# Convolution pieces one slot earlier in an eight-block kernel of convolution and gated network

## The reference

```python
y = irfft(rfft(u, n) * rfft(K, n), n)[..., :L] + u * D
y = y * (arange(L) < length)
q = lambda v: clip(v, -448, 448).astype(float8_e4m3fn).astype(float32)   # all input scales are 1
h = silu(q(y) @ gate_w.T * gate_scale) * (q(y) @ up_w.T * up_scale)      # 512 -> 1376
out = x + q(h) @ down_w.T * down_scale                                   # 1376 -> 512
```

## Time and profile before

| | us |
|---|---|
| median of 3 runs | 326.05 |
| the profiled execution | 326.16 |
| its span | 324.4 |
| TensorE (PE) busy | 310.2 (96%) |
| VectorE (DVE) busy | 303.4 (94%) |
| ScalarE (ACT) busy | 206.3 (64%) |

### The profile page before, as it was taken

The page is one execution under the profiler, slowest core; times in us unless marked ns, Lnnn a source line. Parts: engine busy times, 40 slices in busy tenths (PEclk is TensorE's granted clock), DMA queues, the critical chain, the costliest instruction groups (busy, mean ns, idle before and its releaser), DMA issues.

```text
span 324.4 us, 4763 instructions
## 1 busy us (share of the span) xinstructions
PE 310.2 (96%) x1567; PEld 162.7 (50%) x1593; DVE 303.4 (94%) x464; ACT 206.3 (64%) x318; POOL 12.5 (4%) x20
## 2 busy tenths in 40 slices
PE   1999899999999999999999999999999999989996
PEld 1557554545455554555455544555455454534444
DVE  6989999999999999999998999989998999989784
ACT  4839788278755777476844868366863959364540
POOL 2031000000001000010001000010001000010010
PEclk9999999999999999999999999999999999999999
DMA  5779999400001690077302780067401650051028
GB/s 203 169 179 226 259 277 379 174 1 0 2 0 17 131 359 15 1 129 266 122 0 26 154 337 1 0 116 249 154 0 16 132 242 1 0 100 31 0 34 226
DMA packets 14014, 38.38 MB, mean 118 GB/s; under 512 B 1470, under 2 KB 6558, under 8 KB 11052
## 3 DMA queue, kind: packets, MB, share of 16 engines
q1 hardware_dynamic: 8412, 26.58, 23.1%
q0 software_dynamic: 5584, 11.57, 20.5%
HBM read 33.90 MB, written 15.81 MB: 153 GB/s over the span
## 4 chain that ended last, share of the span: by engine, by line
PE 75%; DVE 16%; issue 4%; ACT 3%; DMA 2%; DVEq 0%; ACTq 0%; SPq 0%
PE gate_ps L535 19%; PE up_ps L535 18%; PE down_ps L491 17%; PE y_ps L477 16%; DVE hv L834 3%; DVE yq L818 3%; DVE yt L807 2%; DVE hq L851 2%; DVE ht L842 2%; PE y_ps L576 1%; DVE ym L799 1%; PE down_ps L576 1%; DMA toep<-kpad_scratch 1%; PE gate_ps L456 1%; PE y_ps L459 1%
## 5 line engine op out<-in xcount | busy, mean ns | idle before, releaser
L392 ACT ACTIVATE sil<-gate_ps,fac 128x512 f32<-128x512 f32 (+1 forms) x88 | 59.7, 680 | 67.8 <-PE gate_ps L535 66.8
L535 PE MATMUL gate_ps<-yq,wg 128*128 128x512 bf16 (+3 forms) x365 | 88.1, 362 | 2.7 <-DVE hv L834 2.4
L535 PE MATMUL up_ps<-yq,wu 128*128 128x512 bf16 (+3 forms) x367 | 88.4, 363 | 0.3
L477 PE MATMUL y_ps<-xt,toep 128*128 128x512 f32 (+3 forms) x256 | 80.4, 434 | 0.5 <-DMA toep<-kpad_scratch 0.5
L491 PE MATMUL down_ps<-wd,hq 128*128 128x512 bf16 (+1 forms) x295 | 76.8, 379 | 0.8
L834 DVE SCALAR_TENSOR_TENSOR hv<-up_ps,fac,sil 128x512 f32<-128x512 f32 (+1 forms) x88 | 65.6, 745 | 8.2 <-ACT sil L392 6.6
L375 ACT ACTIVATE hc<-hv 128x1024 f32<-128x1024 f32 (+1 forms) x48 | 47.1, 980 | 20.9 <-DVE hq L851 19.8
L477 PEld LDWEIGHTS y_ps<-xt,toep 128*128 128x128 f32 x256 | 47.2, 190 | 21.4 <-issue 2.9
L535 PEld LDWEIGHTS gate_ps<-yq,wg 128*128 128x128 bf16 x372 | 35.6, 100 | 43.7 <-ACT sil L392 4.0
L842 DVE SCALAR_TENSOR_TENSOR ht<-hc,hv 128x1024 f32<-128x1024 f32 (+1 forms) x48 | 54.2, 1129 | 1.9 <-ACT hc L375 1.8
L535 PEld LDWEIGHTS up_ps<-yq,wu 128*128 128x128 bf16 x372 | 36.3, 100 | 38.3
(11 more groups left out here) (149 smaller groups left out, 113.0 us busy)
## 6 DMA issues: line engine op xcount, KB each, us to landing
xt<-in_xT SPq DMA_DIRECT2D x8, 1024.0 KB, 7.6
out<-in_x SPq DMA_DIRECT2D x7, 1024.0 KB, 5.7
out<-res POOLq DMA_DIRECT2D x7, 1024.0 KB, 7.8
toep<-kpad_scratch SPq DMA_DIRECT2D x6, 1024.0 KB, 9.8
toep<-kpad_scratch SPq DMA_DIRECT2D x8, 256.0 KB, 4.3
wd<-in_down POOLq DMA_DIRECT2D x1, 1280.0 KB, 21.6
xt<-in_x SPq DMA_DIRECT2D x1, 1024.0 KB, 7.2
out<-xt SPq DMA_DIRECT2D x3, 256.0 KB, 3.1
```

What stands on the lines that cost most here:

```text
L392: nc.scalar.activation(sil[b][0:w, :], gate_ps[b][0:w, :], ACT.Silu, scale=fac[0:w, S_GATE:S_GATE + 1]).then_inc(silu_done, 1)
L477: last = nc.tensor.matmul(y_ps[h % 2][:, d * P:L], toep[par][:, h, d * P:(d + 1) * P], xt[par][:, h, 0:L - d * P], start=(d == 0), stop=(d ...
L535: mm = nc.tensor.matmul(ps[b][0:w, cols], wt[:, k, c * P:c * P + w], yq[par][:, version, k, cols], start=(k == 0), stop=(k == LB - 1))
```

## The change

It moves instructions and alters none:

- `CONV_PLAN`: all pieces of the convolution stand one slot earlier. A block's convolution begins in slot 6 and ends in slot 4; the last piece of channel 1 falls into slot 10, the first of channel 2 into slot 0.
- For block 1 the first piece of channel 2 stands in the start-up, ahead of the last channel's matmuls.
- VectorE: the mask of the first channel two blocks ahead goes from slot 10 to slot 9; the sum of y's last channel from slot 8 to slot 9, behind the tenth product.
- ScalarE: the two copies of K's last group stand before the fourth channel's work of block 0 and not behind it.
- SyncE: the copy of block 0's x is issued behind the loads of block 3.

```diff
--- before.py
+++ after.py
@@ -254,8 +254,8 @@
             load_x_t(2, 0)
             sp.wait_ge(k_stored[2], 16)
             load_toep(2, 0)
+            next_conv(3, 1)
             copy_x(0, 0)
-            next_conv(3, 1)
             copy_x(1, 1)
             with sp.Fori(0, (NBLK - 4) // 2) as j:
                 for par in range(2):
@@ -406,12 +406,13 @@
 
             act.wait_ge(scales_ready, 1)
             for h in range(HB):
+                if h == HB - 1:
+                    copy_k(2)
                 if h:
                     scale_y(0, h)
                 else:
                     act.wait_ge(ym_done, 1)
                 magnitude_y(0, h)
-            copy_k(2)
             scale_y(1, 0)
             magnitude_y(1, 0)
             slots(0, 0, None, True, 2)
@@ -508,7 +509,7 @@
             def beside(g, par, half, c, down, ahead):
 
                 for step, h, distances in CONV_PLAN.get(c, ()):
-                    if step <= ahead and (down or (step, h) != (1, 1)):
+                    if step <= ahead and (down or c):
                         conv(g + step, (par + step) % 2, half + (1 if step == 2 else par), h, distances)
                 if down:
                     down_part(g - 1, 1 - par, c)
@@ -549,6 +550,7 @@
             by_channel(1)
             conv(1, 1, 0, 1, [0, 1, 3, 2])
             by_channel(2)
+            conv(1, 1, 0, 2, [0])
             by_channel(3)
             pe.wait_ge(middle_in, 32)
             slots(0, 0, 0, False, 2)
@@ -910,9 +912,9 @@
                         clip_y(g + 1, 1 - par, ROUND_PLAN[c])
                     if c == 9 and c in plan:
                         rounded(PAIRS * g + plan[c], g, par, plan[c])
+                    if ahead == 2 and c == 9:
+                        mask_y(g + 2, 0)
                     if c == CH - 1:
-                        if ahead == 2:
-                            mask_y(g + 2, 0)
                         if PAIRS - 3 not in plan.values():
                             clip(PAIRS * g + PAIRS - 4, par, PAIRS - 4)
                         rounded_sum(m - 1, PAIRS - 2)
@@ -969,15 +971,14 @@
 
 
 CONV_PLAN = {
-    7: [(2, 0, [0])], 8: [(2, 0, [1, 3])], 9: [(2, 0, [2]), (2, 1, [0])], 10: [(2, 1, [1, 3])],
-    0: [(1, 1, [2])], 1: [(1, 2, [0])], 2: [(1, 2, [1, 3])], 3: [(1, 2, [2]), (1, 3, [0])],
-    4: [(1, 3, [1, 3])], 5: [(1, 3, [2])],
+    6: [(2, 0, [0])], 7: [(2, 0, [1, 3])], 8: [(2, 0, [2]), (2, 1, [0])], 9: [(2, 1, [1, 3])], 10: [(2, 1, [2])],
+    0: [(1, 2, [0])], 1: [(1, 2, [1, 3])], 2: [(1, 2, [2]), (1, 3, [0])], 3: [(1, 3, [1, 3])], 4: [(1, 3, [2])],
 }
 
 MASK_PLAN = {0: 1, 3: 2, 5: 3}
 SCALE_PLAN = {0: (1, 0), 1: (1, 1), 4: (1, 2), 6: (1, 3)}
 MAGNITUDE_PLAN = {1: (1, 0), 2: (1, 1), 5: (1, 2), 7: (1, 3)}
-SUM_PLAN = {2: 0, 3: 1, 6: 2, 8: 3}
+SUM_PLAN = {2: 0, 3: 1, 6: 2, 9: 3}
 ROUND_PLAN = {4: 0, 5: 1, 7: 2, 9: 3}
 H_BEHIND = {3: 0, 7: 1, 10: 2}
 H_EVEN = {3: 0, 7: 1, 9: 2, 10: 3}
```

## The result

The changed kernel takes **335.3** (median of four executions, 333.2 to 337.5) where the kernel before takes 326.06 beside it: ratio 1.0281 [1.0255, 1.0307]. On another chip the same kernel took 333.4 (332.4 to 336.2), ratio 1.0230 [1.0171, 1.0290]. The forecast was 330.9, range 328.4 to 332.4. It had the sign right, and about half of the size: +9.2 measured, +4.8 forecast.

A forecast was written before the change was run, and what follows sets the result against it. TensorE alone was taken to set the steady blocks' length, VectorE to bound block 6, started by TensorE. Terms 2.6 + 1.35 + 0.86 = 4.8 on the profiled 326.16, less 0.1, gave 330.9, range 328.4 to 332.4.

The forecast's parts named there:

- the lower clock: Rival 3, chance 0.05: half clock behind block 2's new wait for one slot's work adds 3.45, giving 334.3.
- blocks 3 to 5: Tile waits of 0.3, 0 and 1.05 from later additions, less the margins; together 1.35, bounds 0 and 2.7.
- Block 2's wait: TensorE in block 2 waits 2.6 for block 4's Toeplitz tile, landing at 124.2; bounds 1.9 and 3.0.
- Start-up: First block's pieces, up to block 2: taken at 0, bounds -1.3 and +0.5.
- The mask wait in block 1: TensorE, near 62, waits 1.7 for the mask of (2, 0) in place of the old 0.6.
- Block 6: All of block 6 shifts by 0.43 + 0.43 = 0.86, bounds 0.4 and 1.0.
- the forecast's step: Block 6's first product waits for TensorE's longer slot 0 piece, 0.86 instead of 0.43, released by ScalarE's silu.
- The first copy's and last taps' new places: ScalarE's two small copies earlier, first copy of x later: both 0, bounds -0.2 and +0.3.
- The tile of block 2: Its store and tile start some 3 earlier, covering its piece in slot 6 of block 0.
- Rival 1: Inputs of blocks 4 to 7 arrive in time, leaving only block 6's 0.86: 326.9, chance 0.08.

The follow-up runs named there:

- the pieces alone: Kernel before with the new `CONV_PLAN`, the start-up piece and the mask in slot 9, nothing else of the change: 331.91, ratio 1.0162.
- The repeat: The changed kernel run again, unaltered, beside its form with TensorE's loop written out, on one chip: 333.38, ratio 1.0230.
- the written-out form: Changed kernel with TensorE's loop over block pairs written out, nothing else: 330.86, ratio 1.0145; again on another occasion 332.37, ratio 1.0211.
- filled: Changed kernel with TensorE's loop written out, plus ten idle matmuls before the tile wait in block 2: 331.16, ratio 1.0149.
- the pieces in their old places: Changed kernel with the convolution pieces back in their old slots, the rest of the change kept: 327.14, ratio 1.0026.
- the eviction moved: Changed kernel with input loads ahead of addition and copy, and ScalarE's first down eviction in slot 5 ahead of its silu: 327.18, ratio 1.0030.
- the loads alone ahead: Changed kernel with SyncE's loop issuing the next input loads ahead of the wait for addition and copy of x: 328.62, ratio 1.0071.
- The unsplit block 6: Kernel before with slot 0 of block 6 working on all four channels at once: 326.14, ratio 1.0000.
- the one closest, with its own loads ahead: Kernel before with SyncE's loop issuing the next input loads ahead of the wait for addition and copy of x: 326.1, ratio 0.9996.

## Why the prediction was right in sign and wrong in size

Three terms failed: the lower clock was put at nothing (1.7 in the profiled execution), blocks 3 to 5 at 1.35 (3.2, beyond their bound of 2.7), and slot 5 was not seen (1.0). The clock alone does not explain the miss: the two of the first four executions with a mean clock of 1.00 took 334.46 and 333.20, above the range's end of 332.4 too.

**Block 2's wait: right.** Addition at 104.5 (forecast about 104), landing 124.7 (124.2), wait 2.44 (2.6). It was 2.60 in the kernel with the pieces alone, too. That the number is so near is in part luck. The addition came 1.55 later and not 1.1, the tile landed after 10.6 and not 9.9, against this the time from the addition's issue to the copy's was 8.19 and not 8.83, and TensorE was ready at 122.33 (120.61 + 2 x 0.86), 0.7 later than forecast. The repeat had 3.13, the written-out form 1.24 and 1.61.

**The clock: put at nothing without a reason.** "I think it unlikely: the core works up to the wait and after it" was no argument. The trace of before showed no wait of that size and said so; a chance of 0.05 was far too low. Measured: of 24 executions of the kernels that wait 1.2 or more for the tile in block 2, or fill that wait (both occasions of the changed kernel 3 of 8, pieces only 2 of 4, written out 2 of 8, filled 0 of 4) seven had a mean clock of 0.995 or less, and of 55 executions of the seven others none was below 0.999. The price was mis-sized in the other direction: 1.7 where 3.45 stood. That the wait is what lowers the clock is argued from these counts and the two profiles, not shown by an experiment: the filling met no lowered execution to mend. The changed kernel's three with the low clock took 336.1 to 337.5, its five others 332.4 to 334.5; that gap of 3.3 between the means holds longer waits and, at 0.990, more lowered stretches, which I did not profile. The Trainium skill, "TensorE: Matmul & The Clock Gate", Part 1, has both sides: an idle engine falls back to half clock, and, of the start of a kernel, how many matmuls run slow differs from run to run of one kernel. The traces agree with the first by the 0.50 behind the wait of 2.44; that the price differs from run to run they show in the middle of the kernel, with 1.7 against 0 behind waits of 2.44 and 3.13.

**Blocks 3 to 5: right mechanism, mis-sized term.** 1.35 was forecast, bounds 0 and 2.7; 3.2 came. The addition's shift was 1.04 on the block's start and 0.43 in work done, 1.47 in place of 1.29. The landing in block 5 was 11.9, 1.0 more than the 10.9 of before on which the term stood. A single landing per block was taken for the value and 0.4 for its spread; the runs show 9.3 to 11.9. By its own working that 0.4 gives bounds of 0.65 and 2.45 and not 0 and 2.7. How much of the excess is the addition's and how much the landing's was not separated.

**Slot 5: left out.** It cost 1.0 in blocks 2 to 5. It could have been read off before anything ran: the plan shows a slot without pieces, and the down group's bank has to be evicted first. Moving the eviction took off 1.44.

**Start-up: 0.5, at its upper bound.** The mask wait in block 1 is 1.79, forecast 1.7. Two things were not carried: VectorE's new order, which costs 0.7 up to block 2 with the pieces in their old places, and slot 5 of block 1, since with the eviction moved only 0.13 is left.

**Block 6: right number, another starter.** 0.86 was forecast, 1.0 was measured for blocks 6 and 7. On TensorE block 6 itself is 0.20 shorter (33.07), and the cost appears in block 7, where TensorE waits 1.06 for a product, 7.13 after the block's start (before 6.37). The first product of block 6, with the pieces alone and in the changed kernel:

```profile
258.55 0.75 DVE L835 SCALAR_TENSOR_TENSOR hv<-up_ps,fac,sil 128x512 f32<-128x512 f32 x1 [1.30 <-ACT sil L392]
```

```profile
261.86 0.75 DVE L836 SCALAR_TENSOR_TENSOR hv<-up_ps,fac,sil 128x512 f32<-128x512 f32 x1
```

With the pieces alone it comes 4.16 after the block's start (254.39), 0.42 later than before, and waits for the silu: this is the forecast's step. In the changed kernel it comes 4.25 after the start, 0.51 later, and VectorE had no idle time before it: VectorE's own list starts it, not TensorE. From this product to the end of TensorE's wait in block 7 it is 35.95, as before (297.81 - 261.86; 287.82 - 251.92 = 35.90). So the 1.0 is 0.43 of work done, 0.51 of a later product and 0.05. That VectorE's list carries it fits the run with the eviction moved, where TensorE's block 6 is 0.23 shorter (32.84) and the wait in block 7 still ends 40.20 after block 6's start (40.19 with the loads alone ahead). The unsplit block 6 does not speak against this: in the kernel before the two lists ran level, so an earlier product won nothing.

**The rest.** The first copy's and last taps' new places left no wait behind, but they were only run with the moved sum and mask, which together cost 1.0. The tile of block 2 was issued 2.2 earlier (37.44, before 39.63), where 3 was forecast. Rival 1's 326.9 is nearly what the kernel takes when the tile waits and slot 5 are gone (327.2). No version here beat the kernel before: the one closest, with its own loads ahead, ties with it.

## What to carry to other kernels

Before moving work forward past a transfer's margin, write down the margin with the spread of the landing in it, not one landing: here 2.59 was taken from margins of 1.1 to 4.0, the blocks lost another 1.5, and every block that fell short paid by itself. When a wait of some microseconds on TensorE is new, price the lower clock as a real case (seven of 24 executions here), not a remote one. And when pieces of work leave a slot, look at who used them as cover: the group behind them will meet a bank that isn't free yet.

## What the runs showed of the hardware

- The same 1 MB tile load lands after 9.3 to 11.9 when a 1 MB copy is issued 1.4 ahead of it, after 8.0 to 9.8 when the copy is issued 0.7 behind it, and after 7.2 to 7.4 when it goes ahead of both addition and copy (the first of the four tiles so loaded, in block 1, after 7.4 to 8.6).
- The granted clock fell to 0.50 for some 3.3 behind a wait of 2.44 in one execution and stayed 1.00 behind 3.13 in another of the same program. The mask wait of 1.79 in block 1 lowered the mean in none of the 16 executions of three kernels that had it without a long tile wait.
- With TensorE's loop written out the landing in the loop's last block was 9.4 to 10.0 in four profiles, against 10.7 to 11.9 in six with the loop. In three of these four the span ended 3.1 to 3.2 behind the start of the last VectorE instruction, in the fourth (filled) and in all ten looped ones 2.6 behind it. Neither is explained.
